# Four transformer stages on one core: the fold's constant rows, value rows and second-batch products are regrouped

## The reference

```
x = x + tanh(g_xattn[0]) * L0_xattn(ctx_1024, layernorm(x), mask, ...)   # latents are x, 4 heads of 64, keys: 1024 rows and 77 context rows
x = x + tanh(g_ffn[0])   * L0_ffn(layernorm(x), ...)                    # spiking feed-forward
x = x + tanh(g_xattn[1]) * L1_xattn(layernorm(x), ctx_1024, ctx_1024, ...)
x = x + tanh(g_ffn[1])   * L1_ffn(layernorm(x), ...)                    # 8 experts

# inside L1_xattn: 16 heads of 64, keys and values from the 77 context rows of a batch
q = (query @ Wq + bq);  k = (key @ Wk + bk);  v = (value @ Wv + bv)
attn = softmax(einsum('bqhd,bkhd->bhqk', q, k) / 8)
out  = einsum('bhqk,bkhd->bqhd', attn, v).reshape(b, sq, 1024) @ Wo + bo + residual
```

## Time and profile before

| | us |
|---|---|
| median of 3 runs (877.62 to 878.11) | 877.65 |
| the profiled execution, its own time | 874.89 |
| its span in the profile | 873.1 |
| TensorE busy in the span | 803.0 (92%) |
| VectorE, ScalarE, GpSimd busy | 544.9, 366.8, 373.0 |
| mean granted clock of TensorE | 0.946 |

### The profile page before, as it was taken

How to read it: one execution, slowest core, us unless ns; L and a number is a source line. 1 busy time by engine, 2 the same in 40 slices (tenths; PEclk the granted TensorE clock), 3 DMA queues, 4 the chain that set the end, 5 groups by cost and what they waited for, 6 DMA issues and landing times.

```text
span 873.1 us, 13817 instructions
## 1 busy us (share of the span) xinstructions
PE 803.0 (92%) x4270; PEld 612.0 (70%) x4271; DVE 544.9 (62%) x1181; ACT 366.8 (42%) x1175; POOL 373.0 (43%) x396
## 2 busy tenths in 40 slices
PE   6888799989999999999999999999998799999995
PEld 4555445555555455558887978888886689999994
DVE  4948775687677857676998667777766333333331
ACT  4547143545354423344444376766660032222220
POOL 6355553354446455355475044444442312222221
PEclk9989597999899979999999999999998799999998
DMA  8670000000000000004600092000001465555420
GB/s 304 184 305 23 1 0 1 1 0 1 1 1 0 1 1 1 0 1 142 225 1 0 1 317 88 18 14 13 14 12 61 116 259 177 179 181 175 175 79 3
DMA packets 31887, 67.14 MB, mean 77 GB/s; under 512 B 3103, under 2 KB 22909, under 8 KB 30813
## 3 DMA queue, kind: packets, MB, share of 16 engines
q1 hardware_dynamic: 28699, 56.17, 18.4%
q0 software_dynamic: 2560, 10.17, 3.5%
q10 hardware_dynamic: 578, 0.19, 0.1%
HBM read 54.74 MB, written 12.68 MB: 77 GB/s over the span
## 4 chain that ended last, share of the span: by engine, by line
PE 69%; DVE 16%; issue 6%; POOL 3%; ACT 3%; DMA 1%; ACTq 0%; DVEq 0%; POOLq 0%
PE PS L2094 9%; PE PS L2106 9%; PE PS L1489 8%; PE PS L735 7%; PE PS L1469 6%; PE PS L1297 5%; PE PS L726 3%; PE PS L1275 3%; DVE row_best L847 3%; PE PS L772 3%; PE PS L702 3%; PE PS L727 3%; POOL rrms L551 2%; PE PS L744 2%; PE PS L1806 1%
## 5 line engine op out<-in xcount | busy, mean ns | idle before, releaser
L1056 ACT ACTIVATE EX<-PS 128x512 f32<-128x512 f32 x144 | 79.0, 594 | 133.2 <-PE PS L727 128.0
L847 DVE TENSOR_REDUCE row_best<-PS 128x1 f32<-128x1024 f32 x64 | 77.8, 1221 | 45.8 <-PE PS L702 45.6
L1016 POOL TENSOR_TENSOR sumP<-sumP,EX 128x1024 f32<-128x1024 f32 x32 | 75.6, 2361 | 39.1 <-ACT EX L1056 38.6
L1671 ACT ACTIVATE pc<-PS,mx 128x77 f32<-128x77 f32 x256 | 78.8, 359 | 26.9 <-DVE mx L1566 26.9
L2094 PEld LDWEIGHTS PS<-xeT,w 128*128 128x128 f32 x736 | 85.6, 192 | 3.5 <-DMA w<-in_L_ffn_W 1.2
L2094 PE MATMUL PS<-xeT,w 128*128 128x128 f32 x736 | 86.1, 275 | 1.9 <-ACT xeT L2056 1.9
L2106 PE MATMUL PS<-w,heT 128*128 x368 | 83.3, 379 | 1.3 <-DVE oe L2036 1.3
L2133 POOL DMA_INDIRECT out<-oe,target x23 | 23.2, 1011 | 125.8 <-DVE oe L2036 125.8
L735 PE MATMUL PS<-EX,V 128*64 128x512 f32 (+1 forms) x288 | 76.6, 641 | 0.0
L2106 PEld LDWEIGHTS PS<-w,heT 128*128 128x128 f32 x368 | 68.1, 190 | 10.0 <-issue 1.7
L1489 PE MATMUL PS<-vw,pcT 128*128 128x256 f32 (+1 forms) x320 | 73.0, 383 | 1.2 <-ACT pcT L1684 1.2
(11 more groups left out here) (283 smaller groups left out, 1715.4 us busy)
## 6 DMA issues: line engine op xcount, KB each, us to landing
w<-in_L_ffn_W SPq DMA_DIRECT2D x31, 1024.0 KB, 5.5
vw_rows<-vwn SPq DMA_DIRECT2D x2, 1232.0 KB
kwH_rows<-kwH SPq DMA_DIRECT2D x1, 2464.0 KB, 7.4
kwL_rows<-kwL SPq DMA_DIRECT2D x1, 2464.0 KB, 13.7
kwH<-kwH_rows POOLq DMA_DIRECT2D x1, 2464.0 KB, 12.4
kwL<-kwL_rows POOLq DMA_DIRECT2D x1, 2464.0 KB, 19.0
vw<-vw_rows SPq DMA_DIRECT2D x2, 1152.0 KB, 13.2
XR<-in_x SPq DMA_DIRECT2D x4, 512.0 KB, 15.0
```

The lines of the kernel that those rows point to most:

```text
L847: dve.tensor_reduce(row_best[:, n % 2, t // GT, t % GT:t % GT + 1], PSf[:, 512 * at:512 * at + S], AX.X, ALU.max, negate=True).then_inc(ma ...
L1016: pool.tensor_tensor(sumP[:], before, EX[:, (KT * n + c) % EB, :, :], ALU.add).then_inc(pool_summed, 1)
L1056: act.activation(EX[0:r, k % EB, i, :], PS[0:r, ST_AT + i, :], ACT.Exp).then_inc(exp_done, 1)
L1671: last = act.activation(pc[:, p, h * C:h * C + C], PS[:, 1 + part, (h - h0) * C:(h - h0) * C + C], ACT.Exp, bias=mx1[:, p, h:h + 1], accum ...
```

## The change

- **Loads.** Wv comes in two halves, each with a semaphore of its own. The first two quarters of x are loaded ahead of Wk and the turned Wq.
- **Constant rows.** GpSimd's two memsets of QA and KA are gone. VectorE writes rows 64 to 99 of each by one copy from a column of the unit matrix that is spread over the row (36 partitions by 4096 and by 4408).
- **Value rows of batch 0.** The odd heads' products go to the ring of banks 0 to 4, and VectorE copies them out, the even heads' stay with banks 5 to 7 and ScalarE.
- **Statistics.** The first two quarters of x are done before `keysT`, the others after chunks 3 and 7. GpSimd does the two powers before it subtracts from the turned Wq.
- **tanh of the gates** moves behind ScalarE's even rows, so ScalarE's first instruction waits for the columns only.
- **Value products of batch 1.** They leave the fold. After each of the eight row scores, `second_values` makes two of them into the two halves of bank 4, and waits for ScalarE's copy of the pair before (`act_second_rows`). Both products of a call use the same 64 rows of the array. Their store comes after the loads of the next stage's weights.
- Wo's buffer moves to a place that is free until later. Two waits on the stores move from ScalarE's start of the attention to its last steps of the first pair, and others guard the first sums on VectorE and GpSimd. Four semaphores are merged or dropped; the stage of the experts is otherwise unchanged.

```diff
@@ pe_attend, dve_attend, pool_attend, act_attend
+            if c == 0:
+                if n > 0:
+                    pe.wait_ge(ot_ready, n)
+                else:
+                    pe.wait_ge(vwo_read, FC + EVEN + SECOND)
...
             row_scores(0, t, MAX_AT if t % 2 == 0 else ST_AT)
+            second_values(pe, t)
             if t % GT == GT - 1:
                 ctx_scores(0, t // GT)
...
+                if (n, c) == (0, KT - 2):
+                    act.wait_ge(spilled, 32)
+                    act.wait_ge(vw_out, 16 * B)
                 numerators(n, c)
@@ new
+    def second_values(pe, j):
+        q, a = j // 2, slice(j % 2 * E0, j % 2 * E0 + E0)
+        if j > 0:
+            pe.wait_ge(vwo_read, FC + EVEN + j)
+        for m in range(2):
+            last = pe.matmul(PS[0:C, SECOND_BANK, m * D:m * D + D], valsT[a, 2 * q + m, 1, :], wo1[a, 2 * q + m, :],
+                             start=True, stop=True)
+        last.then_inc(vwo_done, 1)
+
+    def act_second_rows(act):
+        act.wait_ge(vw_out, 16)
+        rows = vwn[:].rearrange("c (q m a) n -> c q a m n", m=2, a=2)
+        for j in range(SECOND):
+            act.wait_ge(vwo_done, FC + EVEN + j + 1)
+            act.activation(rows[:, j // 2, j % 2], PS[0:C, SECOND_BANK, :].rearrange("c (m n) -> c m n", m=2), ACT.Copy) \
+               .then_inc(vwo_read, 1)
@@ pe_fold
         for h in range(H1):
             if h % 2 == 0:
                 pe.wait_ge(vwo_read, h // 2 + 1)
-            values_times_wo(0, h)
+            values_times_wo((vw_bank, bank)[h % 2], 0, h)
...
-        for h in range(H1):
-            values_times_wo(1, h)
-        pe.wait_ge(vwo_read, FC + B * H1)
-        pe.wait_ge(fold_read, FC + KC * FC)
+        pe.wait_ge(vwo_read, FC + EVEN)
+        pe.wait_ge(fold_read, ODD + FC + KC * FC)
@@ act_fold
+        for h in range(0, H1, 2):
+            k0 = vw_bank.to_read()
+            vw_bank.read(act.activation(vwn[:, h, :], PS[0:C, k0, 0:D], ACT.Copy))
+        act.wait_ge(vec_in, 16 * VECS)
+        act.activation(tg[:], gates[:], ACT.Tanh).then_inc(tanh_ready, 1)
...
-        act.wait_ge(vw_out, 16)
-        copy_rows(1)
@@ dve_fold
+        for h in range(1, H1, 2):
+            k0 = bank.to_read()
+            bank.read(dve.tensor_copy(vwn[:, h, :], PS[0:C, k0, 0:D]))
+        dve_norm(dve, own, [0, 1], False)
...
-            if c % 2 == 1:
-                dve_norm(dve, own, [c // 2], c == FC - 1)
+            if c in (3, FC - 1):
+                dve_norm(dve, own, [2 + c // 4], c == FC - 1)
@@ sp_loads
-        sp.dma_start(wv1[:], t["L1_xattn_Wv"].rearrange("(k p) n -> p k n", p=P)).then_inc(wv_in, 16)
+        sp.dma_start(wv1[:, :, 0:F // 2], wv[:, :, 0:F // 2]).then_inc(wv_in, 16)
+        sp.dma_start(wv1[:, :, F // 2:F], wv[:, :, F // 2:F]).then_inc(wv_rest_in, 16)
         sp.dma_start(wo1[:], t["L1_xattn_Wo"].rearrange("(c p) n -> p c n", p=P)).then_inc(wo_in, 16)
+        for g in (0, 1):
+            load_x(g)
         sp.dma_start(wk1[:], t["L1_xattn_Wk"].rearrange("(k p) n -> p k n", p=P)).then_inc(wk_in, 16)
         sp.dma_start(wqT[:], t["wqT"]).then_inc(wqT_in, 16)
-        for g in range(NG):
+        for g in (2, 3):
             load_x(g)
@@ the streams of pool and vector
-        pool.memset(QA[:].bitcast(F32), 0.0).then_inc(rows_set, 1)
-        pool.memset(KA[:].bitcast(F32), 0.0).then_inc(rows_set, 1)
         pool_rows(pool)
         pool_consts(pool)
+        pool_first_roots(pool)
         pool_query_weights(pool)
...
-        dve.memset(QA[MASKROW:MASKROW + 1].bitcast(F32), 1.0).then_inc(rows_set, 1)
-        dve.memset(KA[SHIFT:SHIFT + GT].bitcast(F32), 1.0).then_inc(rows_set, 1)
+        rows = slice(MASKROW, SHIFT + GT)
+        dve.tensor_reduce(scratch[rows, 5:6], ident[rows, SHIFT:SHIFT + GT], AX.X, ALU.add).then_inc(column_set, 1)
+        dve.tensor_copy(QA[rows].rearrange("p g h n -> p (g h n)"),
+                        ident[rows, MASKROW:MASKROW + 1].to_broadcast([GT + SHIFT - MASKROW, BG * H0 * GN])).then_inc(rows_set, 1)
+        dve.wait_ge(column_set, 1)
+        dve.tensor_copy(KA[rows].rearrange("p h n -> p (h n)"),
+                        scratch[rows, 5:6].to_broadcast([GT + SHIFT - MASKROW, H0 * KPAD])).then_inc(rows_set, 1)
```

More of the change, by code:

```diff
@@ L233, in layers_kernel @@
     wqT = fold.take("wqT", [P, FC, D])
-    wo1 = fold.take("wo1", [P, FC, D])
     keysT = fold.take("keysT", [P, FC, B, 2, C])
@@ L242, in layers_kernel @@
     kwL0 = fold.take("kwL0", [P, KC, B, HK], F32R)
+    wo1 = Region(TOP + 3 * KC * F + 8).take("wo1", [P, FC, D])
+    assert fold.at <= TOP + 3 * KC * F + 8
     top = Region(TOP)
@@ L370, in layers_kernel @@
     VECS = 4
+    ROWS_SET = 7
     ITEMS = S // P + 1
```

80 lines of the change are left out of this document (44 added, 36 removed).

## The result

| | before | after |
|---|---|---|
| median | 877.63 us (6 runs, 873.86 to 878.2) | 884.64 us (6 runs, 882.42 to 886.46) |
| the profiled execution, its own time | 874.89 | 886.46 |
| its span | 873.1 | 884.7 |
| first key scores of the attention | 105.59 us | 118.45 us |

The change makes the kernel slower: the ratio of after to before is 1.0126, 95% interval 1.0092 to 1.016. The medians are 7.0 us apart, 0.8%, the two profiled executions 11.6 us. The six runs of before fall into two groups, 873.9 to 874.3 and 877.6 to 878.2 us, and the medians compare after with the upper one. The prediction was 885.2 us, in a range of 879 to 889.5.

What follows compares the result with a forecast made beforehand. VectorE was taken to bound the fold and nearly the first row scores, where TensorE would become the limit. Fold -3.4 and row scores +10.9 make +7.5 us, on the median 877.65 giving 885.2 us, range 879 to 889.5.

Steps and rivals of the forecast that it cites:

- The fold, -3.4 us: Fold: earlier value products, paired heads and statistics ahead of the keys save 3.4 us, between -4.6 and 0.
- the same bytes stand ahead of it as before, in smaller pieces. I take 13.0: Fold start: Wo lands at 12.8 us, so value products begin at 13.0 instead of 14.42, gaining 1.4 us.
- Hidden, with 1 us to spare: Fold: Wk lands near 18 us, yet enough key banks fill before VectorE reads one at 21.8 us.
- The copies of the constant rows: VectorE's two copies at the fold's start: 4.9 and 5.2 us, half of that as lower bound, not moving 17.7.
- The row scores, +10.9 us: First row scores: added products make TensorE the limit at clock 0.50; 24.4 us to the key scores instead of 13.5.
- the tile, 2.65 us: First row scores: one row score plus two added products per tile on TensorE; eight tiles make 21.2 us.
- A row score takes 0.9: First row scores: TensorE's time per row score at the lower clock, 0.9 us, beside 1.71 us for the products.
- Later, 0: Stages after the first row scores: no change, give or take 2 us for lower-clock stretches in the attention.
- the clock comes back: Rival, chance 0.12: the full clock returns among the row scores, in all -0.6 us, 877.1 us.
- the products hide fully: Rival, chance 0.05: VectorE stays the limit of the row scores, only the fold counts, 874.2 us.
- the fold gains nothing: Rival, chance 0.10: late Wk or turned Wq, or slow row copies, leave only the row scores' cost, 888.6 us.
- three warnings: Signs of error: clock 1.00 between row scores, products' passes under 0.3 us apart, VectorE's first keys after 23 us.

Runs made afterwards that it cites:

- e11: e6 with the value weights Wv loaded in one 1 MB transfer again instead of two halves; ratio to before 0.9931.
- e10: e6 with QA and KA zeroed by GpSimd and their rows of ones set by VectorE memsets, as before the change; ratio to before 0.9983.
- e2: The kernel before with only batch 1's value products moved among the first row scores; ratio to before 1.019.
- e3: The changed kernel with each tile's two batch 1 value products on the two row halves of the array and in banks 4 and 7; ratio to before 1.0078.
- e5: The changed kernel with batch 1's value products on one row half as they are, but in banks 4 and 7 by turns; ratio to before 1.0149.
- e9: The changed kernel with the batch 1 value products repeated as unread filler at the end of the first projection; ratio to before 1.0105.
- e6: e4 with the odd value rows in the fold also copied by ScalarE, none by VectorE; ratio to before 0.9953.
- e12: e6 with Wk issued ahead of the first two groups of x again, as before the change; ratio to before 0.996.
- e1: The changed kernel with batch 1's value products and their copies back at the end of the fold; ratio to before 0.9983.
- e4: The changed kernel with batch 1's value products at the end of the first projection, row halves side by side; ratio to before 0.9979.

## Why the prediction was right, step by step

**The fold, -3.4 us: the mechanism right, the size -1.4.** The step that missed is "the same bytes stand ahead of it as before, in smaller pieces. I take 13.0". The value products began at 14.85 us. Two things stood against 13.0. Wo landed at 14.8 us; e11 shows that the smaller pieces are the reason for some 2 us. And TensorE itself was not done with the first projection before 14.07, which the step left out:

```profile
6.43 7.64 PE L1161 MATMUL PS<-ctxT,wv 128*128 128x154 f32 x32 [6.43 <-DMA wv<-in_L_xattn_Wv]
```

In e11 Wo was there at 12.0 us and the products began at 14.85 all the same. No run began them before 13.70 (e10). From there the steps held with this shift. The pairs of value products were at their floor (3.68 us for 32 passes, 4.4 taken), the two blocks of statistics took 4.1 us, the keys started at 23.16 (21.8) and the normalization came 18.07 us behind them (17.9 by the working). "Hidden, with 1 us to spare" was wrong for Wk: TensorE waited 1.87 us for it until 20.40. Wk was late with Wo: 2 MB behind 14.8 us, at the rate of the rows, end near 20. (1024 KB in 2.6 us are 392 KB per us, not 380; nothing hangs on it.) VectorE was busy until 23.16, so it cost nothing there. The lower clock cost 0.46 us over the turned rows, where 0.3 was taken, and 0.34 at the last turned heads, for which the working had no term. The -1.4 us are those of one pair of profiles: with the normalization at 40.75 to 43.26 us in six profiles of this fold, and at 43.42 and 43.67 in the two of the old one (before, e2), the fold brings between 0.2 and 2.9 us there.

**The copies of the constant rows** were at the lower bound: 2.62 and 2.48 us, not 4.9 and 5.2. Nothing hung on it.

**The row scores, +10.9 us: measured +14.2.** The mechanism is the one that was predicted, and e2, e3, e5 and e9 bear it out: TensorE is the limit at clock 0.50, the wait for the bank costs nothing, and the clock stays low. The term that was mis-sized is the tile, 2.65 us, measured 3.07. "A row score takes 0.9" had been read where passes follow one another; between products its two passes take 1.15, and the four of the products 1.92 and not 1.71. Eight times 0.42 are 3.4 us, all of the difference.

**Later, 0: measured -1.2**, within the 2 us allowed. The "rest" of the table goes from 759.3 to 767.7 us over kernels with the same instructions there, so a difference of this size has no cause that the runs can name.

The sum of the terms as measured is -1.4 + 14.2 - 1.2 = +11.6 us; predicted was +7.5. Two misses of 2.0 and 3.3 us have the same sign. That the medians are 7.0 us apart and the forecast of the median fell within 0.6 us is in part luck: the ratio says +8 to +14 us. On the profiled execution, where the sum was worked out, the forecast was 882.4 us and 886.46 was measured. It met the median because the profiled execution of before lay 2.7 us below its median, and that of after 1.8 us above.

Of the rivals, "the clock comes back" and "the products hide fully" fell with the clock of 0.50 to 125.1 us and with VectorE's waits; "the fold gains nothing" is closer than it looks, since Wo's late landing was its kind of cause. Of the marks named ahead, two of three warnings stayed silent. The third, keys after 23 us, came true by 0.16 us, and rightly pointed at the fold's term. Of the places named, the first row score came at 90.73 us and not near 88.5 (the working's own terms give 88.7), and the key scores 27.7 us behind it and not 24.

## What to carry to other kernels

Ask of a stage not which engine has free time on average, but which would be the limit if the work were added, at the clock that the stage has. Here TensorE was busy 7.11 of 8 us at half clock, and 16 small products cost 14 us, or 8 side by side on the two row halves; side by side in the gaps of 1.3 to 2.4 us ahead of it they cost nothing. Where one engine's queue bounds a stretch (VectorE in the fold), give it no work that an idle one can do, and start it as early as its data allow; then the order and the size of the loads decide next. And look at more than one profile before a place in a stretch that waits for loads is called gained: the same code put the first keys anywhere from 22.7 to 25.2 us.

## What the runs showed of the hardware

- Splitting one load of 1 MB in two delayed the transfers behind it by about 2 us (Wo lands at 14.0 and 12.0 us in e6 and e11; at 14.2 and 12.8 in e12 and before, which have Wo and Wk next to each other alike).
- A wait for a load may cost twice. In three of the six profiles of one fold (e1, e3, e4) TensorE waited 2.1 to 2.2 us in one piece, the clock then read 0.50, and the work behind ran slower (5.37 and not 3.68 us for 32 passes in e1 and e3).
- Work that fills a wait can hold the clock up: with value products before the turned rows eight of these took 1.09 us (e1), without 1.94 (e4, after).
- TensorE was busy 15.97 of 16 us on products over 64 and 65 rows (after, 90.7 to 106.7 us) at a clock of 0.50, and 12.56 of 12.6 us (e3, 92.4 to 105 us) with the value products side by side; in neither did the clock rise.
- Products on the two row halves, in different banks, run side by side at either clock: 16 heads in 3.68 us at 1.00 (after), one after the other in 6.39 (before); four passes within 1.07 us at 0.50 (e3), one after the other within 1.92 (after, e5).
- GpSimd's small instructions are slow beside VectorE's copies of the constant rows. In before, then in after:

```profile
11.37 0.13 POOL L1783 IOTA iotas<- 128x8 f32 x1
```

```profile
4.01 2.23 POOL L1829 IOTA iotas<- 128x8 f32 x1
```

The two copies ran from 3.57 to 8.60 us. This row ends as the first of them does, at 6.2 us; one more, an affine select, takes 2.38 us from 6.37 on and 0.29 in before. Nobody waited for them. In before a VectorE memset of QA's one row lay beside them (10.79 to 14.26 us), and they were fast.
